# Expert FFN of a MetaFormer block in fp32: layer 2 moved from 128x64 to 64x64 TensorE tiles, gelu units shared by two experts

## The reference

```
logits = xt @ Wr + br                      # xt: layer-normed tokens, 8 experts
top_p, top_idx = top_k(softmax(logits), 2); weights = top_p / top_p.sum()
xe = xn * ln_g[e] + ln_b[e]                # xn: xt layer-normed once more
h  = gelu(xe @ W1[e] + b1[e])              # 64 -> 256, all 8 experts
y  = h @ W2[e] + b2[e]                     # 256 -> 64
out = t + sum of weights * y over the two chosen experts
```

## Time and profile before

| | us |
|---|---|
| median of 3 runs | 56.64 (56.33 to 56.64) |
| the profiled execution | 56.28 |
| its span, first to last instruction | 54.5 |
| TensorE busy | 49.7 |
| DVE, ACT, POOL busy | 37.5, 32.0, 18.8 |

### The profile page before, as it was taken

The page is one execution under the profiler, slowest core; times in us unless marked ns, Lnnn a source line. Parts: engine busy times, 40 slices in busy tenths (PEclk is TensorE's granted clock), DMA queues, the critical chain, the costliest instruction groups (busy, mean ns, idle before and its releaser), DMA issues.

```text
span 54.5 us, 2448 instructions
## 1 busy us (share of the span) xinstructions
PE 49.7 (91%) x976; PEld 36.8 (67%) x976; DVE 37.5 (69%) x171; ACT 32.0 (59%) x75; POOL 18.8 (35%) x44
## 2 busy tenths in 40 slices
PE   4999979999968899999999999999999999999900
PEld 2332646976746795597577799896758997599800
DVE  3098689699999795999626899839910319748920
ACT  4600386993796959994499990100699701994000
POOL 4129588000055499996529990000000000000000
DMA  0351366967000000000000000000011000000022
GB/s 0 96 127 19 78 144 137 375 222 268 12 6 0 6 0 0 12 0 0 0 0 18 0 0 12 0 0 12 0 48 48 12 0 0 12 0 6 12 48 48
DMA packets 2940, 2.42 MB, mean 44 GB/s; under 512 B 2032, under 2 KB 2544, under 8 KB 2928
## 3 DMA queue, kind: packets, MB, share of 16 engines
q1 hardware_dynamic: 2608, 2.23, 13.5%
q10 hardware_dynamic: 320, 0.03, 0.5%
HBM read 2.00 MB, written 0.26 MB: 41 GB/s over the span
## 4 chain that ended last, share of the span: by engine, by line
PE 83%; DVE 8%; issue 2%; ACT 1%; DVEq 0%; ACTq 0%
PE banks L960 24%; PE banks L996 22%; PE banks L820 9%; PE banks L1014 7%; PE banks L858 4%; PE banks L937 3%; PE banks L837 3%; PE banks L887 2%; PE banks L902 2%; PE banks L866 2%; PE banks L828 2%; PE banks L845 2%; DVE nmax L529 1%; PE banks L977 1%; DVE res L706 1%
## 5 line engine op out<-in xcount | busy, mean ns | idle before, releaser
L431 ACT ACTIVATE H<-banks,PF 128x512 f32<-128x512 f32 x32 | 19.3, 708 | 7.8 <-PE banks L960 7.3
L960 PE MATMUL banks<-XE,W1F 64*64 64x256 f32 x224 | 13.7, 382 | 0.0
L996 PEld LDWEIGHTS banks<-W2F,H 128*64 128x64 f32 x384 | 11.6, 138 | 1.3 <-issue 1.2
L996 PE MATMUL banks<-W2F,H 128*64 128x64 f32 x384 | 12.2, 223 | 0.0
L960 PEld LDWEIGHTS banks<-XE,W1F 64*64 64x64 f32 x224 | 7.9, 133 | 3.4 <-issue 0.6
L321 POOL TENSOR_SCALAR XE<-XF,PF,LB 128x256 f32<-128x256 f32 x14 | 7.8, 567 | 1.6 <-ACT XF L409 1.6
L820 PE MATMUL banks<-const-bfloat16-1.0 128*128 128x512 bf16 x11 | 4.9, 615 | 0.8 <-PEq L1124 0.8
L299 POOL TENSOR_TENSOR rs<-base,half 128x2 f32<-128x2 f32 x4 | 2.8, 701 | 6.9 <-DVE base L570 6.8
L392 ACT ACTIVATE PR<-banks,nmax 128x256 f32<-128x256 f32 x8 | 3.8, 481 | 1.3 <-DVE nmax L529 1.2
L658 DVE TENSOR_TENSOR prod<-banks,gate 128x512 f32<-128x512 f32 x4 | 2.8, 690 | 2.3 <-PE banks L996 2.3
L1014 PEld LDWEIGHTS banks<-W2F,H 128*64 128x64 f32 x128 | 3.9, 138 | 0.5 <-issue 0.4
(11 more groups left out here) (81 smaller groups left out, 69.4 us busy)
## 6 DMA issues: line engine op xcount, KB each, us to landing
W1F<-in_w_dram SPq DMA_DIRECT2D x1, 768.0 KB, 4.5
W2F<-in_w_dram SPq DMA_DIRECT2D x1, 512.0 KB, 4.7
W1F<-in_w_dram SPq DMA_DIRECT2D x1, 256.0 KB, 3.4
X<-in_x_dram SPq DMA_DIRECT2D x2, 64.0 KB, 1.9
X<-in_x_dram SPq DMA_DIRECT2D x1, 128.0 KB, 2.3
B2D<-in_b_dram SPq DMA_DIRECT2D x8, 2.0 KB
out_dram<-res SPq DMA_DIRECT2D x1, 128.0 KB, 1.7
out_dram<-res SPq DMA_DIRECT2D x2, 64.0 KB, 1.8
```

The source lines that it names most:

```text
L431: nc.scalar.activation(H[:, r, :].rearrange("p (t n) -> p t n", t=PT), ps_z[z_slot(g // J)][:, :, PIX * j:PIX * j + PIX], ACT.Gelu, bias=P ...
L960: mm = nc.tensor.matmul(ps_z[z_slot(q)][C * c:C * c + C, k, PIX * j:PIX * j + PIX], W1F[rows, e, j, C * c:C * c + C], XE[h][rows, e, :], s ...
L996: mm = nc.tensor.matmul(ps_y[s % 2][C * c:C * c + C, k, n, :], H[:, (2 * J * s + J * k + j) % RING, left:left + C], W2F[:, J * (2 * p + k) ...
```

## The change

A gelu's 128 partitions now hold 64 hidden numbers of expert 2p and 64 of expert 2p + 1. Layer 1 gets that by giving its two column tiles the weights and inputs of two experts. Unit q is then half f = q % 2 of the pair p. Layer 2 goes on 64x64 tiles: row tile r holds the 64 hidden numbers of expert 2p + r, so the row chooses the expert, and each row tile writes its own bank. A step takes 128 passes of 64 rows where it took 64 passes of 128 rows. It reads its four gelus one after the other for each tile of tokens.

The results of layer 2 now take two banks each (`ps_y`, `ps_tail`), which are banks 4, 5 or 2, 3, so layer 1 goes round two bank pairs instead of three from unit 4 on. The last two transpositions, the gates and the bias become four 64x64 products each. W2 is transferred in four parts, and b1 a second time, in four small parts, in the order of the new gelus (`B1`). The order on TensorE, DVE and POOL changes, and with it what some steps wait for.

```diff
-def z_before(q):
-    return {1: 0, 2: 0, 9: 7, 10: 8}.get(q, q - 3)
 def z_slot(q):
-    return (0, 1, 2, 3, 1, 2, 3, 1, 2, 1, 2, 3, 1, 2, 3, 1)[q]
+    return q if q < 4 else 1 + q % 2
...
-        ps_y = [banks[:, 4 + k, :].rearrange("p (k n c) -> p k n c", k=2, c=C) for k in range(2)]
-        ps_tail = [[banks[:, bank, C * (n % 2):C * (n % 2) + C] for n, bank in enumerate(used)]
-                   for used in ((4, 4, 5, 5), (6, 6, 7, 7), (4, 4, 5, 5), (6, 7, 0, 1))]
+        ps_y = [banks[:, k:k + 2, 0:PIX] for k in (4, 4, 2, 4, 2, 4)]
+        ps_tail = [[banks[:, k:k + 2, C * (n % 2):C * (n % 2) + C] for n, k in enumerate(used)]
+                   for used in ((2, 2, 4, 4), (2, 0, 6, 4))]
...
-            sp.dma_start(W2F[:, :, :], w2).then_inc(w2_in, 16)
+            for r in range(2):
+                for f in range(2):
+                    sp.dma_start(W2F[C * r:C * r + C, :, f, :, :],
+                                 w2[C * f:C * f + C, :, :].rearrange("q (p r j) c -> q p r j c", r=2, j=J)[:, :, r, :, :])\
+                        .then_inc(w2_in, 16)
+            for r in range(2):
+                for f in range(2):
+                    sp.dma_start(B1[C * r:C * r + C, :, f, :],
...
             def turn_x2(i):
...
                 if i >= IMG:
-                    pe.wait_ge(t_ready, IMAGES)
+                    pe.wait_ge(h_ready, J * 4)
+                    for t in range(PT):
+                        for r in range(2):
+                            rows = slice(C * r, C * r + C)
+                            nc.tensor.matmul(ps_x2[i][C * t:C * t + C, r, :], X2[i // IMG][rows, n + t, :],
+                                             ident[rows, rows], start=True, stop=True).then_inc(x2_ps, 1)
+                    return
...
             def layer1_first(q, i):
                 pe.wait_ge(w1_in[0], 16)
+                pe.wait_ge(xe_first, i + 1)
+                pe.wait_ge(xe_second, i + 1)
...
             def layer1(q):
...
-                if q > 3:
-                    pe.wait_ge(h_ready, J * (z_before(q) + 1))
-                if q == 11:
-                    pe.wait_ge(base_ready, HALVES)
+                else:
+                    pe.wait_ge(h_ready, J * (q - 2 if q < 6 else q - 1))
                 for j in range(J):
-                    for c in range(2):
-                        for k in range(PT):
-                            rows = slice(C * k, C * k + C)
+                    for k in range(PT):
+                        rows = slice(C * k, C * k + C)
+                        for c in range(2):
                             mm = nc.tensor.matmul(ps_z[z_slot(q)][C * c:C * c + C, k, PIX * j:PIX * j + PIX],
-                                                  W1F[rows, e, j, C * c:C * c + C], XE[h][rows, e, :],
+                                                  W1F[rows, 2 * p + c, j, C * f:C * f + C], XE[h][rows, 2 * p + c, :],
...
             def layer2(s):
                 p = s % PAIRS
-                pe.wait_ge(w2_in, 16)
+                pe.wait_ge(w2_in, 64)
                 if s == 0:
-                    pe.wait_ge(h_ready, J)
-                if s == 1:
+                    pe.wait_ge(t_ready, IMAGES)
+                elif s == 2:
                     pe.wait_ge(scaled_ready, HALVES)
-                if s > 1:
-                    pe.wait_ge(prod_ready, s - 1)
-                for k in range(2):
-                    pe.wait_ge(h_ready, J * (2 * s + k + 1))
-                    for n in range(TILES):
-                        for j in range(J):
+                elif s == 3:
+                    pe.wait_ge(base_ready, HALVES)
+                else:
+                    pe.wait_ge(prod_ready, {1: 1, 4: 3, 5: 4}[s])
+                for n in range(TILES):
+                    for x in range(2 * J):
+                        if n == 0:
+                            pe.wait_ge(h_ready, 2 * J * s + x + 1)
+                        for r in range(2):
+                            rows = slice(C * r, C * r + C)
                             for c in range(2):
                                 left = P * n + C * c
-                                mm = nc.tensor.matmul(ps_y[s % 2][C * c:C * c + C, k, n, :],
-                                                      H[:, (2 * J * s + J * k + j) % RING, left:left + C],
-                                                      W2F[:, J * (2 * p + k) + j, :],
-                                                      start=(j == 0), stop=(j == J - 1))
+                                mm = nc.tensor.matmul(ps_y[s][C * c:C * c + C, r, C * n:C * n + C],
+                                                      H[rows, (2 * J * s + x) % RING, left:left + C],
+                                                      W2F[rows, p, x // J, x % J, :],
+                                                      start=(x == 0), stop=(x == 2 * J - 1))
...
+            def layer2_tail(t):
+                s = STEPS - 2 + t
+                if t == 0:
                     pe.wait_ge(prod_ready, STEPS - 2)
+                pe.wait_ge(h_ready, 2 * J * (s + 1))
                 for n in range(TILES):
+                    if t == 1 and n in (0, 3):
+                        pe.wait_ge(tail_ready, TILES if n == 0 else 2 * TILES)
+                    for x in range(2 * J):
```

More of the change, by code:

```diff
@@ L111, in build_block @@
         LB = sb("LB", [P, E])
-        B2D = sb("B2D", [HALVES * TILES * E, TILES, C])
+        B2D = sb("B2D", [P, TILES, C])
+        B1 = sb("B1", [P, PAIRS, 2, J])
         W1F = sb("W1F", [P, E, J, P])
-        W2F = sb("W2F", [P, UNITS, C])
+        W2F = sb("W2F", [P, PAIRS, 2, J, C])
         ident = sb("ident", [P, P])
@@ L797, in _ @@
             weigh(1)
+            weigh(2)
+            add_bias(0)
+            add_bias(1)
             add_up(1)
-            weigh(2)
             add_up(2)
             weigh(3)
-            add_bias(0)
-            add_bias(1)
             add_up(3)
@@ L811, in _ @@
             add_base()
-            for k in range(4):
-                for n in range(TILES):
-                    weigh_tail(k, n)
+            for n in range(0, TILES, 2):
+                for k in range(2):
+                    weigh_tail(0, n, k)
+                    weigh_tail(0, n + 1, k)
+            weigh_tail(1, 0, 0)
+            weigh_tail(1, 1, 0)
+            weigh_tail(1, 0, 1)
+            weigh_tail(1, 2, 0)
+            weigh_tail(1, 1, 1)
+            weigh_tail(1, 2, 1)
+            weigh_tail(1, 3, 0)
+            weigh_tail(1, 3, 1)
         @block.tensor
@@ L967, in turn_gates @@
                 pe.wait_ge(gate_ready, HALVES)
-                pe.wait_ge(h_ready, J * 7)
-                nc.tensor.transpose(ps_gates, gate[:, :, :, :].rearrange("p h t e -> p (h t e)"), ident[:, :])\
-                    .then_inc(gates_ps, 1)
+                pe.wait_ge(prod_ready, 2)
+                for r in range(2):
+                    rows = slice(C * r, C * r + C)
+                    for c in range(2):
+                        nc.tensor.matmul(ps_gates[C * c:C * c + C, r, :],
+                                         gate[rows, :, :, :].rearrange("p h t e -> p (h t e)"), ident[rows, rows],
+                                         start=True, stop=True).then_inc(gates_ps, 1)
             def bias():
@@ L975, in bias @@
                 for h in range(HALVES):
-                    rows = slice(TILES * E * h, TILES * E * h + TILES * E)
-                    nc.tensor.matmul(ps_bias[h].rearrange("p n c -> p (n c)"), gateT[rows, :],
-                                     B2D[rows, :, :].rearrange("p n c -> p (n c)"), start=True, stop=True,
-                                     tile_position=(TILES * E * h, 0)).then_inc(bias_ps, 1)
+                    rows = slice(C * h, C * h + C)
+                    for c in range(2):
+                        nc.tensor.matmul(ps_bias[h][C * c:C * c + C, :, :].rearrange("p n c -> p (n c)"), gateT[rows, c, :],
+                                         B2D[rows, :, :].rearrange("p n c -> p (n c)"),
+                                         start=True, stop=True).then_inc(bias_ps, 1)
@@ L1061, in _ @@
             logits(1)
+            layer2(1)
             layer1(7)
+            layer2(2)
             layer1(8)
-            layer2(1)
-            layer2(2)
             turn_gates()
+            layer1(9)
+            bias()
+            layer1(10)
             layer2(3)
-            bias()
-            layer1(9)
-            layer1(10)
             layer1(11)
+            layer2(4)
             layer1(12)
-            layer2(4)
+            layer1(13)
             layer2(5)
-            layer1(13)
             layer1(14)
             layer1(15)
-            for k in range(4):
-                layer2_tail(k)
+            layer2_tail(0)
+            layer2_tail(1)
 _OUTS = [((P, IMAGES * PT, C), 'float32')]
```

111 lines of the change are left out of this document (56 added, 55 removed).

## The result

| | before | after |
|---|---|---|
| median | 56.48 us (56.10 to 56.64) | 67.06 us (66.12 to 67.12) |
| ratio after / before, 95% interval | | 1.185 (1.177 to 1.193) |
| profiled execution, span | 56.28, 54.5 us | 67.05, 64.7 us |
| passes of TensorE | 976 | 1513 |
| TensorE busy | 49.7 us | 50.5 us |

Some executions of a kernel are over 1.5% longer than its fastest; the ratio leaves them out, the median does not.

A forecast was written before the change was run, and what follows sets the result against it. The prediction took TensorE's sequence as the bound: waits of 2.8 us plus 0.2 for a second dependent product at the end, less 2.2 gained, gave +0.80 us, 57.08 profiled and a median of 57.3 us, range 55.8 to 58.8.

The forecast's parts named there:

- the price of a step of layer 2: Layer 2: 128 passes on four tiles at 14.6 ns take 1.87 us a step, so layer 2 itself gains nothing.
- rival 2: TensorE is not fed a layer 2 step's 256 instructions: 9 to 10 ns each, 60 to 62 us; chance 0.10.
- The gain from the changes of shape: TensorE from layer 2's first step on: fewer tile shape changes save 2.2 us if it runs without waits.
- (a): Layer 1's first product also waits for expert 1's input from POOL, starting at 18.77, not 18.36: +0.41 us.
- (b): The transposition after layer 2's first step waits for gelu 7: +0.14 us.
- (c): Unit 6 of layer 1 reuses unit 4's banks and waits for its two gelus: +0.76 us of idle TensorE.
- (d): The bias waits for ScalarE's copy of the gates, which stands behind gelus 16 and 17: +0.89 us.
- (e): Step 3 of layer 2 waits for the two additions that read the bias out of its banks: +0.22 us.
- (f): The tail's second half waits for four DVE products to free its first banks: +0.37 us.
- rival 1: The waits mostly hide because ScalarE gets to its work early enough: 1.65 us shorter, 55.65 us; chance 0.14.
- rival 3: Shape changes are not gone or layer 1 loses: units 5% dearer add 0.6 us, 57.9 us; chance 0.08.
- The floor of about 25 ns: Skill's least spacing of matmul starts: 3.2 us a layer 2 step, about 11 us more; the prediction rejected it.

The follow-up runs named there:

- experiment 1: Kernel before plus four unread streams of 1024 TensorE instructions each (tiny bf16, new layer 2 form, its 128-column version, old form): 111.95 us, streams 13.9 to 14.9 us each.
- experiment 5: Kernel before plus 512 passes of layer 2's new form written out, then 1024 of the same passes as a TensorE loop: 84.68 us, one execution.
- experiment 6: Kernel before with only the third transposition, gates and bias as small products in neighbours' shapes, layer 2 kept old: 55.60 us, ratio 0.987.
- experiment 3: Changed kernel without row tile 1 in layer 2 and its tail, half of layer 2's instructions: 58.20 us, ratio 1.029 to the kernel before.
- experiment 2: Changed kernel with 32 tiny products more and 3 long ones fewer in TensorE's warm-up, 58 instructions more: 67.33 us.

## Why the prediction was wrong

**The step that failed** is the price of a step of layer 2, 1.87 us: the sum put the time to get its 256 instructions to TensorE at nothing. In its place the runs showed 256 new instructions in 3.45 to 4.0 us, and pauses of 9.4 us in sum. The prediction had this as rival 2, priced at 9 to 10 ns an instruction, 60 to 62 us, with a chance of 0.10. As it put it, "nothing shows that the supply holds; at 14 ns a step would last 3.6 us". That is the right mechanism and nearly the right number: 13.5 to 15.6 ns in experiments 1 and 5. I then took a lower price because of the router's 32 instructions in 0.20 us. A burst of 32 lies within one block and says what the array can start; it says nothing on how fast blocks of 256 come. The row that says more was there: two steps of old layer 2, 256 instructions in 3.88 us, 15 ns each. No 128 passes in a row of the kernel before take under 3.79 us, so nothing there showed that a block can be had faster. The full 14 us did not come; the likely reason, from the counts, is that units of layer 1 (32 instructions in 0.86 us, 27 ns each) and waits lie between the steps and need fewer instructions than come meanwhile. From 25.40 on, some 2380 instructions take 36.1 us, 15.1 ns each: the second half as a whole runs at the supply's rate. The sign that the prediction named for rival 2, a step of 2.2 us or more, came at every step that had a pause in it: 44.25 to 47.10, for one.

**Layer 2's own work** came as forecast, 1.89 us a step (1.87), 14.8 ns a pass (14.6). So the work of the step was priced rightly; what was missing is what the step waits for.

**The gain from the changes of shape** is there: layer 2 starts 0.91 us after the unit of 22.45 does, where it was 1.03, and nothing is late between layers 1 and 2. In experiment 6 the small products alone brought 0.8 us (56.44, the median of before beside it, less 55.60).

**The waits.** (a) The first product starts at 18.71 (18.77 forecast). (b) is hidden in a pause. (c) and (d) are released by ScalarE, as written. From start to start (c) is 0.71 us (0.76 forecast). (d) is 1.07 and (e) 0.49; an undisturbed unit needs 0.17 of that from its last product to the next block (44.08 to 44.25), so the waits are 0.90 (0.89 forecast) and 0.32 (0.22). (f) does not appear, since a pause of TensorE in front of the tail's second half gives DVE time; in experiment 3, where no pause is, TensorE idles 0.5 there. Neither long wait was hidden by an early ScalarE, so rival 1 fell. An undisturbed unit took 0.87 us (43.38 to 44.25), so rival 3 fell too.

**The sum.** DVE's last product ends at 62.59, 9.7 us behind my 52.93: 9.4 of pauses, 0.5 less for (b) and (f), and 0.8 more in small pieces. Of these, 0.1 is (e), some 0.2 the steps at 1.89 and not 1.87 us, and 0.25 lies between TensorE's last product and DVE's last (1.1 us where I had 0.84); the rest I can't place. Around the span lie 2.35 us (67.05 less 64.7) and not 1.8, but only in the profiled execution: in the other three it is 1.9 to 2.0.

The blocks have a name: the Trainium skill (Runtime: NRT & Kernel Launch, "Instruction fetch mechanics") says that an engine's instructions are refilled in blocks of 16 KiB and that crossing into a new one is mostly hidden. The blocks are in this trace, 16384 bytes a packet and 256 instructions apart; but here the crossings are hidden only while a block holds at least some 3.5 to 4 us of work. Below that each costs up to 2.3 us (experiment 1). The floor of about 25 ns from start to start, which the prediction cited from the Trainium skill (TensorE: Matmul & The Clock Gate, "Wait — 56ns, not 53.3ns?"), is none for passes on four tiles (14.8 ns each in the loop). As a mean over code that is written out it comes out nearly right, 27 to 29 ns a pass in experiment 1, for another reason: by it I had worked out +11 us, and +10.6 came, which is luck. I was right that the router's row speaks against the rule and wrong to stop there.

## What to carry to other kernels

A change that keeps TensorE's work and doubles its instructions is not free: count new instructions per us over stretches of several hundred, not over a burst. Here, written-out code got 256 instructions (128 fp32 passes) in 3.5 to 4 us; a kernel whose densest long stretch is already at 14.6 ns an instruction has next to nothing left. Pauses of TensorE with the releaser "issue", whole blocks of 256 instructions apart and in the middle of any stage, are its sign; a loop whose instructions are already there does not have them, at 0.15 us a round. Products that stand alone between two shapes are worth putting into a neighbour's shape by themselves (1.3% here, for three of them).

## What the runs showed that I had not expected

- Fetches of TensorE's instructions overlapped little: in the second half a packet was asked for 1.1 to 1.5 us after TensorE had gone on, took 0.95 to 1.35 us, and TensorE went on 1.3 to 1.6 us after it had landed. That these add up to the 3.8 us is read from the times; what asks for a packet was not tried.
- On 128x64 tiles a pass of 32 columns took 29.6 ns and one of 64 columns 29.2: the columns are not what it costs. That it is the weight load, the same 128x64 in both, is only argued. The supply would come to nearly the same number, but wherever it was the limit it showed as pauses, and here there are none.
- A jump back in a loop of TensorE cost 0.15 us.
- Left open: why the packet for the first pause (0.81 us, behind pass 334) was asked for at 21.47 us in experiment 2 and at 22.88 in the changed kernel; that it landed earlier fits the missing pause. What sets the time of a block, 3.4 to 4.2 us in the changed kernel, is open too. And the pauses were taken away only together with instructions or by a loop; a faster fetch was not tried.
